# Recurrent mixer: joins and first substitutions over the filled rows only, without clearing the update tiles

## The chip, the cores and the metric

The kernel runs on one core of a Trainium2 chip. The metric is the device time of one execution in microseconds (us). The engines are named as in the profile: PE (TensorE matmuls), PEld (its weight loads), DVE (VectorE), ACT (ScalarE), POOL (GpSimd) and SP (SyncE, whose queue issues the DMAs; SPq in the rows).

## What is computed

The program is a whole two-layer model on 32 samples of 114 positions (1 class token, 36 image patches, 77 text tokens) with 256 channels: a text encoder, a recurrent mixer, routed experts, a state mixer and a factorised MLP. Only the recurrent mixer matters here. Its reference is a scan over the positions:

```python
mixed = silu(causal_conv4(hidden @ W_qkv.T));  z = hidden @ W_z.T
beta = sigmoid(hidden @ W_b.T);  g = -exp(A_log) * softplus(hidden @ W_a.T + dt_bias)
def step(Sst, inp):                     # per sample and head, Sst is 64 x 64
    q_t, k_t, v_t, g_t, b_t = inp
    Sst = Sst * exp(g_t)
    delta = (v_t - Sst.T @ k_t) * b_t
    Sst = Sst + outer(k_t, delta)
    return Sst, Sst.T @ q_t
out = rmsnorm(o * silu(z)) * norm_weight @ W_out.T
```

There are 8 key heads, 16 value heads and 64 channels per head.

## The kernel before, in words

The scan isn't run step by step. For each sample and head the kernel builds a 114x114 triangular matrix `nt` of decayed key products and solves a triangular system for the updates (`upd`, in the code `x`); the outputs are then one product with the decayed query products `qd`.

The system is solved by blocks of 32 rows (the last has 18). The inverses of the four diagonal blocks of all heads and both samples of a pair (128 blocks) are found on DVE at once, one block per partition, in `ue`, by 30 steps of elimination (`eliminate`, L1248 and L1250: a product into `elim_tmp` and a subtraction). Two diagonal blocks are then joined into one inverse of 64 (or 50) rows: `join` (L1665) multiplies the part of `nt` beside the blocks by a turned inverse that lies in `x`; DVE copies the result into `zs` (`join_read`, L1268); `inverse` (L1678) multiplies by the other inverse; ACT copies it into `ut` (`inverse_read`, L1490). Then come the right sides and the substitutions (`solve`): the first halves, rows 0 to 63 (L1700, 64 columns of weights), the carry of their solution into the second halves (L1690), the second substitutions over rows 64 to 113 (L1700, 50 columns), and the outputs (L1707). ACT copies each of them out of PSUM (L1482, L1498).

In `join`, the two joins of a head are issued in turn: one writes PSUM rows 32 to 63 and the other rows 96 to 113 of the same bank. Both, and the first substitution and the carry too, contract over all 114 rows, so what isn't filled in `x` and `zs` has to be zero. For that POOL clears both `x` tiles (`clear_x`, L1196) and DVE clears a gap in them after the join reads (L1272), and SP's loads of the turned inverses into `x` wait for POOL's clearing (`x_clear`). `CHAINS` are the four groups of eight heads (two samples, two groups), each with PSUM banks of its own.

The order of the work is written out by hand: every engine runs `iteration(p)` for each pair of samples `p` (16 pairs, and two more turns of the pipeline), and semaphores alone couple the engines. In one iteration pair `p` forms its matrices, pair `p-1` is eliminated and solved, pair `p-2` is gated, multiplied by `w_out` and stored, and pair `p+1` is projected and convolved.

- DVE: elimination steps with the units of `nt` and `qm` (L1280, L1287) and the gating of `p-2` (L1295, L1300, L1306) between them; turning of the inverse (L1260); gate products (L1311); join reads; the convolutions `conv` 0 to 3 (L1322), with `silu` (L1329) before the last; four products `gated` (L1335).
- ACT: decays (L1414, L1425), reads of the projections, first taps of the convolutions (`first_tap`, L1452: 0 and 1 before the joins, 2 after the reads of the first substitutions, 3 after those of the second), the copies above, `tanh` (L1458).
- PE: projections (L1601), key products (L1576) and decays (L1589), `output_turn` (L1626) and `output_product` (L1634) of `p-2`, gate products (L1617), turning of the values (L1648), then `join`, `inverse`, `solve`.
- POOL: `query_decay` 0 and 1 (L1187), `gate_power` twice (L1200), `clear_x` twice, `query_decay` 2 to 7, and at the end `mask_blocks` on `ue` (L1206, L1210).
- SP: stores the eliminated blocks to DRAM and loads them back in the layouts of `x` (L1133) and `ut` (L1139).

Of the kernel before, what the change touches and what calls it, by code (L numbers as in the profile page):

```python
# [1014 lines left out]
def delta_net(c, hid, xts):  # L1015
# [14 lines left out]
    with ExitStack() as ctx:  # L1030
        def sb(name, shape, dt=F32):
# [23 lines left out]
         o_mm, og_r, osq_r, ms_r, rms_r, on_r, ot_mm, oT_r, wo_mm, h_r, d_dve, pe_gate, pool_gate, sp_gate, x_clear,  # L1055
         uet_r, vd_out, u_in, zz_mm, zs_r, ww_mm, wr_r, x_gap) = (
# [5 lines left out]
                "ms_ready", "rms_ready", "on_ready", "ot_mm", "oT_ready", "wo_mm", "h_ready", "dve", "pe_gate", "pool_gate", "sp_gate", "x_cleared",  # L1062
                "inverse_turned", "turned_out", "turned_in", "join1_mm", "join1_ready", "join2_mm", "join2_ready", "x_gap_cleared"))
# [23 lines left out]
        with nc.Block() as block:  # L1087

            @block.sync
            def _(sp):  # L1090
# [19 lines left out]
                def iteration(p, a=True, proj=True, z=True, d=True):  # L1110
# [10 lines left out]
                    if z:  # L1121
# [7 lines left out]
                        sp.wait_ge(x_clear, r.n * 2 + 2)  # L1129
# [48 lines left out]
            def _(pool):  # L1178
# [34 lines left out]
                def iteration(p, a=True, proj=True, z=True, d=True):  # L1213
                    r = p.shift(-2)
                    for v in range(4):
                        if a:
                            query_decay(p, 2 * v)
                            query_decay(p, 2 * v + 1)
                        if d and v == 0:
                            gate_power(r, 0)  # L1220
                            gate_power(r, 1)
                        if z and v == 0:
                            clear_x(p.shift(-1), 0)
                            clear_x(p.shift(-1), 1)
                    if a:
                        mask_blocks(p)
# [12 lines left out]
            def _(dve):  # L1239
# [23 lines left out]
                def join_read(r):  # L1263
                    for m, (s, g) in enumerate(CHAINS):
                        dve.wait_ge(zz_mm, r.n * 4 + m + 1)
                        need(dve, ww_mm, r.n * 4 - 3 + m)
                        for _, rows, _ in JOINS:
                            last = dve.tensor_copy(zs[s][rows, hs(g), :], ps[rows, XBANK[m], 0:256].rearrange("p (h c) -> p h c", h=8))  # L1268
                        last.then_inc(zs_r, 1)
# [4 lines left out]
                def unit(p, v):  # L1274

                    s, u = divmod(v, 2)
# [5 lines left out]
                    if v == 0:  # L1282
                        need(dve, p_mm, p.n * 4 - 4)
                        need(dve, nd_out, p.n * 128 - 128)
                    for o in range(2):
                        dve.wait_ge(e_r, p.n * 8 + 2 * v + o + 1)
                        dve.tensor_tensor(  # L1287
                            nt[p.par][s][:, hs(u), :].rearrange("p (a o b) t -> p a o b t", o=2, b=2)[:, :, o],
                            e[o][:, :, :].rearrange("p (a b) t -> p a b t", b=2),
                            kq[:, o, :, 1, :].unsqueeze(2).to_broadcast([S, 2, 2, S]), ALU.mult).then_inc(nt_r, 1)  # L1290
# [22 lines left out]
                def conv(r, n):  # L1313

                    dve.wait_ge(tap_r, r.n * 4 + n + 1)
                    for k in range(1, TAPS):
                        for i in range(4):
                            t = 4 * n + i
                            y = yqk[:, t, :, :] if t < 8 else yv[r.par][:, t - 8, :, :]
                            if k > 1:  # L1320
                                dve.wait_ge(conv_r, r.n * 48 + 12 * n + 4 * (k - 2) + i + 1)
                            dve.scalar_tensor_tensor(y, raw[:, t, :, k:k + S], taps[:, t, k:k + 1], y, ALU.mult, ALU.add).then_inc(conv_r, 1)  # L1322
# [14 lines left out]
                def iteration(p, a=True, proj=True, z=True, d=True):  # L1337
# [3 lines left out]
                    if a:  # L1341
                        unit(p, 0)
# [5 lines left out]
                    if a:  # L1348
                        unit(p, 1)
# [9 lines left out]
                    if a:  # L1359
                        unit(p, 2)  # L1360
                    if z:
                        eliminate(r, 20, BW - 1)
# [6 lines left out]
                    if a:  # L1369
                        unit(p, 3)  # L1370
# [3 lines left out]
                    if z:  # L1374
                        join_read(r)
                    if proj:
                        conv(nxt, 0)
                        conv(nxt, 1)
                        conv(nxt, 2)
                        silu(nxt, 0)  # L1380
                        conv(nxt, 3)
# [4 lines left out]
                    if z:  # L1386
                        for m in range(1, 4):
                            gated(r, m)
# [15 lines left out]
            def _(act):  # L1404
# [13 lines left out]
                def decay_terms(p, v):  # L1418

                    s, u = divmod(v, 2)  # L1420
                    for o in range(2):
                        need(act, dec_mm, p.n * 8 + 2 * v + o - 1)
                        for m in range(4):
                            head = 8 * u + 4 * (m // 2) + 2 * o + m % 2
                            last = act.activation(gl[o][:, m, :], c.upto[:, :], ACT.Copy,  # L1425
                                                  scale=gates[:, bass.ds(p.sample(s), 1), head:head + 1].rearrange("p a h -> p (a h)"))
                        last.then_inc(gl_r, 1)
# [46 lines left out]
                def rhs_read(r, q):  # L1474
                    rows = HALVES[q]
                    for m, (s, g) in enumerate(CHAINS):
                        if q == 0:
                            act.wait_ge(vt_mm, r.n * 4 + m + 1)
                            act.wait_ge(zz_mm, r.n * 4 + m + 1)
                        else:  # L1480
                            act.wait_ge(p_mm, r.n * 4 + m + 1)
                        act.copy(x[s][rows, hs(g), :], ps[rows, VBANK[m], :].rearrange("p (h d) -> p h d", h=8)).then_inc(rc_r, 1)  # L1482

                def inverse_read(r):

                    for m, (s, g) in enumerate(CHAINS):
                        act.wait_ge(ww_mm, r.n * 4 + m + 1)
                        need(act, t_mm, r.n * 8 - 3 + m)
                        for rows, cols, _ in JOINS:
                            last = act.copy(ut[s][rows, hs(g), cols],  # L1490
                                            ps[rows, XBANK[m], 256:].rearrange("p (h c) -> p h c", h=8)[:, :, 0:cols.stop - cols.start])
                        last.then_inc(wr_r, 1)

                def x_read(r, q):
                    rows = HALVES[q]
                    for m, (s, g) in enumerate(CHAINS):
                        act.wait_ge(t_mm, r.n * 8 + 4 * q + m + 1)
                        act.copy(x[s][rows, hs(g), :], ps[rows, XBANK[m], :].rearrange("p (h d) -> p h d", h=8)).then_inc(xc_r, 1)  # L1498

                def iteration(p, a=True, proj=True, z=True, d=True):  # L1500
                    r, done, nxt = p.shift(-1), p.shift(-2), p.shift(1)

                    def raws(lo, hi):
                        if proj:
                            for f in range(lo, hi):
                                raw_read(nxt, f)

                    def exps(v):
                        if a:
                            decay_exp(p, 2 * v)  # L1510
                            decay_exp(p, 2 * v + 1)
                            if v < 3:
                                decay_terms(p, v + 1)

# [3 lines left out]
                    exps(0)  # L1518
                    raws(0, 4)
                    exps(1)  # L1520
                    raws(4, 6)
# [3 lines left out]
                    exps(2)  # L1525
                    raws(6, 8)
# [3 lines left out]
                    exps(3)  # L1530
# [3 lines left out]
                    if proj:  # L1534
                        decay_terms(nxt, 0)
                        first_tap(nxt, 0)
                        first_tap(nxt, 1)
                    if z:
                        rhs_read(r, 0)
                        inverse_read(r)  # L1540
                        x_read(r, 0)
# [1474 lines left out]
```

## Time and profile before

| | |
|---|---|
| median of 3 runs | 3087.56 us (3084.33 to 3089.98) |
| profiled execution | 3085.63 us |
| its span in the trace | 3083.9 us |
| PE, DVE, ACT, POOL busy in the span | 79%, 68%, 40%, 26% |
| mean granted PE clock | 0.881 |

The mixer's iterations lie between about 880 and 2160 us of the span. Busy shares are averages over all stages; the profile's clock is a share of the full 2.4 GHz, of which two levels are granted, 1.00 and 0.50 (1.2 GHz). A granted clock between them in a row is a mean over a stretch that had both. In a timeline row the bracket is the idle time of that engine before the row and what ended it. A float32 matmul of the code is two MATMUL records, so the 64 matmuls of the joins are x128. Times in the rows are from the start of the span.

### The profile page before, as it was taken

How to read it: one execution, taken by the hardware profiler on the slowest of the kernel's cores; microseconds unless marked ns; L12 is line 12 of the kernel's file. 1: busy time of each engine (PE TensorE's matmuls, PEld its weight loads, DVE VectorE, ACT ScalarE, POOL GpSimd, SP SyncE). 2: the span in 40 equal slices, each digit the busy share in tenths (PEclk: the TensorE clock that was granted, in tenths of full speed). 3: DMA queues.
4: the chain of work that ended last, by engine and by line, in shares of the span. 5: the costliest groups of instructions: out<-in, count | busy, mean ns of one | idle time of the engine just before them, and what ended most of it. 6: DMA issues, size and time to landing. Idle time of an engine off the chain costs nothing. (4 is left out here: it accounts for less than half of the span.)

```text
span 3083.9 us, 53608 instructions
## 1 busy us (share of the span) xinstructions
PE 2436.0 (79%) x19286; PEld 1864.6 (60%) x19286; DVE 2084.8 (68%) x5004; ACT 1244.2 (40%) x2990; POOL 815.8 (26%) x644
## 2 busy tenths in 40 slices
PE   7888887997458888888888888876452847889698
PEld 5666665886446666666666666655341735566454
DVE  4777774333368888888888888855563336876663
ACT  1334342221256566666666666642000213344132
POOL 2111100001033232232222333221377036450110
PEclk9999998997579999999999999988665877899799
DMA  4210001002201111211122211111211852110000
GB/s 141 72 62 27 12 9 45 21 27 75 100 19 46 49 49 49 50 49 50 49 50 49 50 49 49 46 46 30 88 45 21 263 176 63 45 51 4 18 25 25
DMA packets 274346, 169.01 MB, mean 55 GB/s; under 512 B 182847, under 2 KB 250318, under 8 KB 273728
## 3 DMA queue, kind: packets, MB, share of 16 engines
q1 hardware_dynamic: 247949, 140.28, 15.9%
q0 software_dynamic: 26112, 25.03, 3.1%
q8 instruction: 166, 2.72, 0.4%
q14 instruction: 119, 0.97, 0.1%
HBM read 99.23 MB, written 73.45 MB: 56 GB/s over the span
## 5 line engine op out<-in xcount | busy, mean ns | idle before, releaser
L1187 POOL TENSOR_TENSOR qd<-decay,qm 114x456 f32<-114x456 f32 x128 | 143.4, 1141 | 638.3 <-DVE qm L1280 492.5
L1601 PE MATMUL d_ps<-d_xT,w_qkv 128*128 128x228 f32 x1024 | 236.8, 391 | 44.7 <-DVE qmask L1395 29.2
L1601 PEld LDWEIGHTS d_ps<-d_xT,w_qkv 128*128 128x128 f32 x1024 | 217.2, 213 | 77.1 <-issue 43.2
L2256 POOL DMA_INDIRECT s_eo<-rows_y,slots_all x128 | 152.4, 1191 | 148.3 <-POOLq L87 110.3
L1248 DVE TENSOR_TENSOR elim_tmp<-ue 128x30 f32<-128x30 f32 (+14 forms) x480 | 178.8, 372 | 13.8
L1250 DVE TENSOR_TENSOR ue<-ue,elim_tmp 128x30 f32<-128x30 f32 (+14 forms) x480 | 171.9, 358 | 16.5
L475 PE MATMUL t_ps<-xT,w_qk 128*128 128x154 f32 x1024 | 151.1, 300 | 40.3 <-DVE qk L308 30.9
L1589 PE MATMUL d_ps<-gl,after 114*114 114x456 f32 x256 | 137.2, 654 | 47.2 <-DVE sz L1335 47.2
L1322 DVE SCALAR_TENSOR_TENSOR y_v<-raw,taps,y_v 128x228 f32<-128x228 f32 x384 | 167.1, 508 | 10.6 <-ACT y_v L1452 10.5
L475 PEld LDWEIGHTS t_ps<-xT,w_qk 128*128 128x128 f32 x1024 | 136.7, 189 | 51.8 <-DVE qk L308 38.1
L1206 POOL TENSOR_SCALAR_AFFINE_SELECT ue<-ue 128x1024 f32<-128x1024 f32 x16 | 98.6, 6162 | 238.1 <-DMA ue<-blocks_n 238.1
L1414 ACT ACTIVATE decay<-d_ps,gates 114x114 f32<-114x114 f32 x512 | 133.1, 372 | 64.9 <-PE d_ps L1589 64.5
L1847 POOL DMA_INDIRECT rows_x<-r_xn,slot x128 | 144.3, 1128 | 51.1 <-issue 36.7
L1322 DVE SCALAR_TENSOR_TENSOR y_qk<-raw,taps,y_qk 128x228 f32<-128x228 f32 x384 | 142.2, 450 | 22.0 <-ACT y_qk L1452 21.6
L1425 ACT ACTIVATE gl<-upto,gates 114x114 f32<-114x114 f32 x512 | 151.6, 416 | 0.0
L1634 PE MATMUL d_ps<-w_out,oT 128*114 128x256 f32 x512 | 126.9, 404 | 16.3 <-ACT oT L1471 16.3
L1700 PE MATMUL d_ps<-upd,ut 114*50 114x64 f32 (+1 forms) x2048 | 130.5, 227 | 2.9 <-issue 2.4
L1700 PEld LDWEIGHTS d_ps<-upd,ut 114*50 114x50 f32 (+1 forms) x2048 | 126.5, 138 | 6.2 <-issue 5.7
L1617 PE MATMUL d_ps<-w_z,d_xz 128*114 128x512 f32 x256 | 121.4, 619 | 10.7 <-DVE sz L1311 9.6
L1634 PEld LDWEIGHTS d_ps<-w_out,oT 128*114 128x114 f32 x512 | 95.9, 190 | 46.5 <-ACT oT L1471 20.6
L276 POOL TENSOR_TENSOR rstd<-rstd,minus_half 77x1 f32<-77x1 f32 x32 | 23.4, 732 | 377.2 <-DVE rstd L291 377.2
L415 ACT COPY pT<-t_ps 77x462 f32<-77x462 f32 (+1 forms) x96 | 44.8, 498 | 191.2 <-PE t_ps L525 186.5
(343 smaller groups left out, 5625.0 us busy)
## 6 DMA issues: line engine op xcount, KB each, us to landing
rows_x<-zero_row SPq DMA_DIRECT2D x4, 2048.0 KB, 7.7
ue<-blocks_n SPq DMA_DIRECT2D x16, 512.0 KB, 4.9
blocks_u<-ue SPq DMA_DIRECT2D x16, 512.0 KB, 2.6
blocks_v<-on SPq DMA_DIRECT2D x16, 512.0 KB, 2.7
e_x<-rows_x SPq DMA_DIRECT2D x32, 256.0 KB, 4.3
e_gu<-L_ffn_w_gate_up SPq DMA_DIRECT2D x32, 256.0 KB, 4.3
rows_y<-e_y SPq DMA_DIRECT2D x32, 256.0 KB, 3.4
blocks_n<-nt SPq DMA_DIRECT2D x96, 64.0 KB
```

Source lines behind the costliest of these rows:

```text
L475: last = pe.matmul(ps[:, 6 + f % 3 % 2, (t - lo) * P2:(t - lo + 1) * P2], w_qk[:, k, t * 128:(t + 1) * 128], xT[pair % 3][:, k, :], start= ...
L1187: pool.tensor_tensor(qd[p.par][s][:, hs(u), :].rearrange("p (a o b) t -> p a o b t", o=2, b=2)[:, :, o], e[o][:, :, :].rearrange("p (a b) ...
L1248: ch(dve.tensor_tensor(part, ue[:, j, j + 1:].unsqueeze(1).to_broadcast([128, j, BW - 1 - j]), ue[:, 0:j, j:j + 1].to_broadcast([128, j, B ...
L1250: step = dve.tensor_tensor(ue[:, 0:j, j + 1:], ue[:, 0:j, j + 1:], part, ALU.subtract)
L1322: dve.scalar_tensor_tensor(y, raw[:, t, :, k:k + S], taps[:, t, k:k + 1], y, ALU.mult, ALU.add).then_inc(conv_r, 1)
L1425: last = act.activation(gl[o][:, m, :], c.upto[:, :], ACT.Copy, scale=gates[:, bass.ds(p.sample(s), 1), head:head + 1].rearrange("p a h -> ...
L1589: pe.matmul(ps[0:S, 4 + o, 0:4 * S].rearrange("p (h t) -> p h t", h=4), c.after[:, :], gl[o][:, :, :], start=True, stop=True).then_inc(dec ...
L1601: last = pe.matmul(ps[:, f % 2, (t % 2) * W:(t % 2 + 1) * W], w_qkv[:, k, t * 128:(t + 1) * 128], xT[:, k, :], start=(k == 0), stop=(k == ...
L1634: last = pe.matmul(ps[0:S, 6, 0:D], oT[:, k, :], w_out[:, k, :], start=(k == 0), stop=(k == 7))
L1700: last = pe.matmul(ps[rows, XBANK[m], i * DH:(i + 1) * DH], ut[s][:, 8 * g + i, rows], x[s][:, 8 * g + i, :], start=True, stop=True)
L1847: pool.indirect_dma_start(out=rows_x, out_offset=bass.IndirectOffsetOnAxis(ap=slot[g % 3][:, s, k:k + 1], axis=0), in_=xn[g % 3][:, s, :], ...
L2256: pool.indirect_dma_start(out=eo[n % EO][:, s * TOPK + k, :], out_offset=None, in_=rows_y, in_offset=bass.IndirectOffsetOnAxis(ap=slots_al ...
```

## The change

- `join` becomes `join_part`: each of the two joins of a head contracts only over the 32 rows that are filled (rows 0 to 31, or 64 to 95). The eight matmuls of one join of a group follow each other, and the other join follows later, behind a wait for the first one's end.
- The first substitutions and the carries contract over rows 0 to 63 alone (`known`, `HALVES[0]`). The inverse's second product, the second substitutions and the outputs are as before.
- `clear_x` on POOL and the clearing of the gap on DVE, with their semaphores, are gone. SP's loads into `x` wait for the outputs of the pair before (`o_mm`) instead.
- Everything else in the diff writes loops out by hand in the order that they had.

```diff
 # SP
-                        sp.wait_ge(x_clear, r.n * 2 + 2)
+                        need(sp, o_mm, r.n * 4)
 # POOL
-                def clear_x(r, s):
-                    need(pool, o_mm, r.n * 4 - 2 + 2 * s)
-                    pool.sem_inc(pool_gate, 1)
-                    pool.memset(x[s][:, :, :], 0.0).then_inc(x_clear, 1)
 # DVE, end of join_read
-                    for s in range(2):
-                        rows, _, o = JOINS[1]
-                        dve.memset(x[s][rows, :, o:o + BW], 0.0).then_inc(x_gap, 1)
 # PE
-                        for i in range(8):
-                            for _, rows, o in JOINS:
-                                last = pe.matmul(ps[rows, XBANK[m], i * BW:(i + 1) * BW], nt[r.par][s][:, 8 * g + i, rows],
-                                                 x[s][:, 8 * g + i, o:o + BW], start=True, stop=True)
-                        last.then_inc(zz_mm, 1)
+                def join_part(r, m, n):
+                    s, g = CHAINS[m]
+                    lower, rows, o = JOINS[n]
+                    for i in range(8):
+                        last = pe.matmul(ps[rows, XBANK[m], i * BW:(i + 1) * BW], nt[r.par][s][lower, 8 * g + i, rows],
+                                         x[s][lower, 8 * g + i, o:o + BW], start=True, stop=True)
+                    last.then_inc(zz_mm if n else za_mm, 1)
+                def join_second(r, m):
+                    pe.wait_ge(za_mm, r.n * 4 + m + 1)
+                    pe.sem_inc(pe_gate, 1)
+                    join_part(r, m, 1)
+                # substitute(r, q, m)
+                    known = HALVES[0] if q == 0 else slice(0, S)
+                        last = pe.matmul(ps[rows, XBANK[m], i * DH:(i + 1) * DH], ut[s][known, 8 * g + i, rows],
+                                         x[s][known, 8 * g + i, :], start=True, stop=True)
+                # carry(r, m)
+                        last = pe.matmul(ps[HALVES[1], VBANK[m], i * DH:(i + 1) * DH], nt[r.par][s][HALVES[0], 8 * g + i, HALVES[1]],
+                                         x[s][HALVES[0], 8 * g + i, :], start=False, stop=True, skip_group_check=True)
+                # order on PE
+                        join_first(r, 0, a)
+                        join_first(r, 1, a)
+                        join_second(r, 0)
+                        join_second(r, 1)
+                        join_first(r, 2, a)
+                        join_first(r, 3, a)
+                        join_second(r, 2)
+                        join_second(r, 3)
```

`JOINS` is `[(slice(0, 32), slice(32, 64), 0), (slice(64, 96), slice(96, 114), 32)]`.

## Rows read from the trace of the kernel before

**Rows 1.** Windows, one iteration: busy time and records by engine, granted clock.

```profile
1223.80:1301.90 78.10, 67.08 (x705) 53.04 (x704) 68.25 (x151) 48.35 (x125) 21.59 (x14) 0.94 0.20 49
```

**Rows 2.** Timeline of that iteration, from the elimination's end to the inverse.

```profile
1259.83 0.21 DVE L1250 TENSOR_TENSOR ue<-ue,elim_tmp 128x30 f32<-128x30 f32 x1
...
1264.23 1.91 SPq L1133 DMA_DIRECT2D upd<-blocks_v  x4
...
1269.12 2.18 PE L1665 MATMUL d_ps<-upd,nt 114*32 114x32 f32 x128 [1.01 <-DMA upd<-blocks_v]
1269.92 3.54 DVE L1268 COPY join<-d_ps 32x256 f32<-32x256 f32 x8 [2.52 <-PE d_ps L1665]
...
1273.62 1.03 DVE L1272 MEMSET upd<- 32x512 f32 x2 [0.16 <-issue]
1274.12 3.30 PE L1678 MATMUL d_ps<-ut,join 114*32 114x32 f32 x128 [2.82 <-DMA ut<-blocks_u]
```

**Rows 3.** Timeline, its substitutions and the convolutions beside them.

```profile
1277.35 4.06 PE L1700 MATMUL d_ps<-upd,ut 114*64 114x64 f32 x61
...
1281.40 3.57 PE L1690 MATMUL d_ps<-upd,nt 114*50 114x64 f32 x61
...
1282.11 1.61 ACT L1452 ACTIVATE y_v<-raw,taps 128x228 f32<-128x228 f32 x4
...
1283.75 6.21 DVE L1322 SCALAR_TENSOR_TENSOR y_v<-raw,taps,y_v 128x228 f32<-128x228 f32 x12 [0.19 <-ACT y_v L1452]
...
1284.81 3.74 PE L1700 MATMUL d_ps<-upd,ut 114*50 114x64 f32 x64
...
1291.85 4.47 DVE L1322 SCALAR_TENSOR_TENSOR y_v<-raw,taps,y_v 128x228 f32<-128x228 f32 x12
```

**Rows 4.** Waits between 1000 and 1800 us (ten iterations): total, times, longest.

```profile
DVE y_v L1322 <- ACT y_v L1452: 8.3, 7, 5.0
```

**Rows 5.** Timeline, POOL's clearing and what follows it on POOL, DVE and PE.

```profile
1237.12 1.84 POOL L1196 MEMSET upd<- 114x1024 f32 x2
...
1238.92 2.75 POOL L1187 TENSOR_TENSOR qd<-decay,qm 114x456 f32<-114x456 f32 x2
...
1239.47 1.27 DVE L1248 TENSOR_TENSOR elim_tmp<-ue 128x234 f32<-128x234 f32 x1
...
1240.78 1.16 DVE L1250 TENSOR_TENSOR ue<-ue,elim_tmp 128x234 f32<-128x234 f32 x1
1241.97 0.41 DVE L1248 TENSOR_TENSOR elim_tmp<-ue 128x238 f32<-128x238 f32 x1
...
1241.55 3.71 PE L1634 MATMUL d_ps<-w_out,oT 128*114 128x256 f32 x16 [0.94 <-ACT oT L1471]
...
1245.77 0.41 DVE L1306 TENSOR_TENSOR d_h<-d_h,d_ps 114x256 f32<-114x256 f32 x1
```

**Rows 6.** Timeline, text attention: matmuls with PSUM rows 0 and 64 in turn.

```profile
318.08 1.30 PE L537 MATMUL t_ps<-pT,v 77*64 77x77 f32 x32
```

**Rows 7.** Timeline, last stage: 128 and 16 rows contracted, 456 columns streamed.

```profile
2952.37 1.71 PE L2902 MATMUL f_ps<-f_xT,f_in 128*128 128x456 f32 x4
2955.73 1.79 PE L2910 MATMUL f_ps<-f_aT,f_c 16*128 16x456 f32 x4
...
2931.02 3.40 PE L2910 MATMUL f_ps<-f_aT,f_c 16*128 16x456 f32 x4
```

**Rows 8.** Windows: PE first, granted clock third from the end.

```profile
2930.20:2933.40 3.20, 3.20 (x6) 1.30 (x5) 0.69 (x1) 0.46 (x1) 0.00 (x0) 0.50 0.28 83
...
1274.70:1277.90 3.20, 3.20 (x108) 3.16 (x103) 3.20 (x9) 2.33 (x8) 0.00 (x0) 0.50 0.63 138
...
1039.20:1049.20 10.00, 7.77 (x138) 7.54 (x134) 8.22 (x23) 3.60 (x10) 3.29 (x2) 0.50 0.42 137
```

**Rows 9.** Timeline of the iteration in which the clock stayed low longest.

```profile
1043.91 6.20 PE L1700 MATMUL d_ps<-upd,ut 114*64 114x64 f32 x61
...
1052.45 4.49 DVE L1322 SCALAR_TENSOR_TENSOR y_v<-raw,taps,y_v 128x228 f32<-128x228 f32 x12 [5.03 <-ACT y_v L1452]
```

More of the change, by code:

```diff
@@ L1213, in iteration @@
                 def iteration(p, a=True, proj=True, z=True, d=True):
[L1214 to L1224, printed above, removed]
-                    if a:
+                    r, done, nxt = p.shift(-1), p.shift(-2), p.shift(1)
+                    if a:
+                        query_decay(p, 0)
+                        query_decay(p, 1)
+                    if d:
+                        gate_power(done, 0)
+                        gate_power(done, 1)
+                    if a:
+                        query_decay(p, 2)
+                        query_decay(p, 3)
+                        query_decay(p, 4)
+                        query_decay(p, 5)
+                        query_decay(p, 6)
+                        query_decay(p, 7)
                         mask_blocks(p)
@@ L1386, in iteration @@
                     if z:
-                        for m in range(1, 4):
-                            gated(r, m)
+                        gated(r, 1)
+                        gated(r, 2)
+                        gated(r, 3)
                     ch.end()
@@ L1472, in oT_read @@
                                        ACT.Copy, scale=gain[:, :]).then_inc(oT_r, 1)
[L1474 to L1498, printed above, removed]
+                def rhs_read(r, q, m):
+                    rows, (s, g) = HALVES[q], CHAINS[m]
+                    if q == 0:
+                        act.wait_ge(vt_mm, r.n * 4 + m + 1)
+                        act.wait_ge(zz_mm, r.n * 4 + m + 1)
+                    else:
+                        act.wait_ge(p_mm, r.n * 4 + m + 1)
+                    act.copy(x[s][rows, hs(g), :], ps[rows, VBANK[m], :].rearrange("p (h d) -> p h d", h=8)).then_inc(rc_r, 1)
@@ L1669, in inverse @@
-                def inverse(r):
-                    for m, (s, g) in enumerate(CHAINS):
-                        if m == 0:
-                            pe.wait_ge(ut_in, r.n * 128 + 128)
-                        pe.wait_ge(zs_r, r.n * 4 + m + 1)
-                        pe.sem_inc(pe_gate, 1)
-                        for i in range(8):
-                            for rows, cols, _ in JOINS:
-                                last = pe.matmul(ps[rows, XBANK[m], 256 + i * BW:256 + i * BW + cols.stop - cols.start],
-                                                 zs[s][:, 8 * g + i, :], ut[s][:, 8 * g + i, cols], start=True, stop=True)
-                        last.then_inc(ww_mm, 1)
@@ new lines, in value @@
+                def value(r, m, a):
+                    s, g = CHAINS[m]
+                    if m == 0:
+                        pe.wait_ge(yy_r, r.n * 2 + 2)
+                    if s:
+                        pe.wait_ge(sz_r, r.n * 4 + 3 + g)
+                    elif a:
+                        pe.wait_ge(e_r, r.n * 8 + 15 + g)
+                    else:
+                        need(pe, og_r, r.n * 4 - 3 + g)
+                    for t in range(4):
+                        last = pe.matmul(ps[0:S, VBANK[m], t * 128:(t + 1) * 128], yv[r.par][:, 4 * g + t, s, :], c.ident[:, :],
+                                         start=(t == 0), stop=True, is_transpose=True, skip_group_check=True)
+                    last.then_inc(vt_mm, 1)
@@ new lines, in join_second, with inverse @@
+                def join_second(r, m):
+                    pe.wait_ge(za_mm, r.n * 4 + m + 1)
+                    pe.sem_inc(pe_gate, 1)
+                    join_part(r, m, 1)
+                def inverse(r, m):
+                    s, g = CHAINS[m]
+                    if m == 0:
+                        pe.wait_ge(ut_in, r.n * 128 + 128)
+                    pe.wait_ge(zs_r, r.n * 4 + m + 1)
+                    pe.sem_inc(pe_gate, 1)
+                    for i in range(8):
+                        for rows, cols, _ in JOINS:
+                            last = pe.matmul(ps[rows, XBANK[m], 256 + i * BW:256 + i * BW + cols.stop - cols.start],
+                                             zs[s][:, 8 * g + i, :], ut[s][:, 8 * g + i, cols], start=True, stop=True)
+                    last.then_inc(ww_mm, 1)
@@ new lines, in outputs @@
+                def outputs(r, m):
+                    s, g = CHAINS[m]
+                    if m == 0:
+                        pe.wait_ge(qd_r, r.n * 8 + 8)
+                        pe.sem_inc(pe_gate, 1)
+                    pe.wait_ge(xc_r, r.n * 8 + 4 + m + 1)
+                    for i in range(8):
+                        last = pe.matmul(ps[0:S, VBANK[m], i * DH:(i + 1) * DH], qd[r.par][s][:, 8 * g + i, :],
+                                         x[s][:, 8 * g + i, :], start=True, stop=True)
+                    last.then_inc(o_mm, 1)
```

361 lines of the change are left out of this document (214 added, 147 removed).

## Prediction

> **What bounds the kernel now.** I read the windows of one iteration first, then its timeline, then the waits. In 78.1 us DVE is busy for 68.3 and PE for 67.1 [rows 1], so neither engine is full, and the question is which waits come last in an iteration. The elimination ends on DVE at 1260.04; the blocks go to DRAM and come back, the joins start 9.1 us later (the DMA into `upd` ends PE's wait) and the inverse 14.1 us later (the DMA into `ut` ends a wait of 2.8 us) [rows 2]. After the first substitutions ACT reads, makes the first tap of convolution 2, and DVE starts that convolution 0.03 us behind it, having waited 0.19 [rows 3]. In ten iterations DVE waits there 7 times, 8.3 us in all [rows 4]. So two paths from the elimination's end reach convolution 2 at nearly the same time: DVE's own (join reads, clearing, convolutions 0 and 1) and DMA, inverse, first substitutions, ACT. Saving on one of them alone saves little; lengthening the second is paid in full. From convolution 2 to the next elimination's end it is DVE's own work that counts, with convolution 3 waiting in the same way for the second substitutions: it starts 3.3 us after they end [rows 3], of which reads and tap on ACT take about 2.7.
>
> **The clearing, and SP's wait.** POOL's two clearings end at 1238.96, and the load into `upd` is issued at 1264.23, when the stored blocks have landed [rows 2, 5]: the load waits for something else, and the outputs of the pair before, for which it is to wait now, are older still. No gain, no cost. Two clearings of the gap take DVE 1.03 us, with the gap ahead of them 1.2 [rows 2].
>
> What POOL does 1.84 us sooner is `query_decay` 2 and 3 [rows 5]. Behind them two elimination steps took 1.27 and 1.16 us where the next took 0.41: 1.6 us lost while POOL read SBUF. Earlier by up to 1.8 us, these two overlap units that read PSUM and the scaling of the gated outputs instead. I expect one of the two collisions to remain. But DVE then meets another wait: the residual (L1306) needs `output_product`, which ends at 1245.26, only 0.5 us before the residual starts today, and whose own start (the scaling) doesn't move. So the gain is between 0 and 0.5 us; I take 0.3, over 14 iterations 4 us. The Trainium skill ("SBUF — State Buffer", section "Who interferes with whom") says that a DVE instruction with two SBUF inputs contends with a GpSimd instruction that reads SBUF and not with one that only writes; the trace agrees, with 1.16 to 1.27 us beside `query_decay` against 0.41. By it alone, with no residual to wait for, the term would be 1.6 x 14 = 22 us.
>
> **The joins.** The contraction over fewer rows saves no time by itself: four matmul records of 456 columns take 1.79 us with 16 rows and 1.71 us with 128 [rows 7]. The order costs. Today two places of PSUM rows alternate, and a record takes 2.18/128 = 17 ns, 0.53 ns a column; the attention, with two places in turn, has 1.30/32 = 41 ns for 77 columns, also 0.53 [rows 2, 6]. The carries, all in one place, take 3.57/61 = 59 ns for 64 columns, 0.91 ns [rows 3]. The new joins write one place eight times in a row: 32 x 0.91 = 29 ns a record, 128 of them 3.7 us instead of 2.2. The ends are 2.2 (no loss) and 7.4 (29 ns doubled at the low clock). At 3.7 PE still ends 1.3 us before `ut` arrives. DVE's first read needs 48 records instead of 32 and comes some 0.8 us later, the last ends about 0.95 later; with 1.2 less for the clearing DVE is 0.25 us ahead at convolution 2, where it waits for ACT anyway: 0 now, at most 0.25 x 16 = 4 us if ACT were in time. The wait for the first join's end has eight matmuls of another group before it and costs nothing. Substitutions and carries keep their columns and records: no change at the same clock.
>
> **PE's clock.** This is the term that decides. The inverse's 3.30 us fell in a stretch at 0.50 (1.2 GHz), after PE had mostly waited for `ut` [rows 2, 8]; the clock is low there in about half of the iterations and is back for the substitutions. The inverse contracts over 114 rows. What the clock did when PE was busy with few rows is shown in the last stage: at 2930.2 to 2933.4 PE was busy without a gap, from 2931.0 on with records of 16 rows, and the clock stayed at 0.50, the four records taking 3.40 us instead of 1.79 [rows 7, 8]. I conclude that few rows count for little in what lifts the clock or holds it. After the change PE has, before the inverse, 3.7 us of 32-row joins between two waits, and behind it 7.6 us of 64-row matmuls. So I expect the clock to fall in or before the inverse in every iteration, and, unless the inverse alone lifts it at once, to stay low through substitutions and carries, up to the second substitutions with their 114 rows.
>
> The trace has one iteration to price that by: the clock was at 0.50 from 1039.2 to 1049.2, 61 records of the first substitutions took 6.20 us, 102 ns each, and DVE waited 5.03 us at convolution 2 [rows 8, 9]. In terms of the iteration of rows 2 and 3: the inverse ends at 1277.4 as now; first substitutions 64 x 102 ns = 6.5, to 1283.9 (now 1281.4); convolution 2 at 1286.2 (+2.5). Carries slowed by the same 102/58: 6.5 us, to 1290.4; second substitutions, at the low clock for two thirds of their way, 5.6 us, to 1296.0 (now 1288.5); ACT 2.7 us; convolution 3 at 1298.7 instead of 1291.85. That is +6.8, less a little that DVE saves because POOL's masking no longer falls beside convolution 2: 6.5 us for an iteration in which the clock stays low. Where it comes back with the inverse, the start of the fall within the joins still costs 0 to 1.3 us; I take 0.5. How many are of each kind depends on where the fall starts, which differs from one iteration to the next; since it starts earlier than today, before the inverse rather than over it, I take 10 of the 16 as staying low.
>
> **Sum.** 10 x 6.5 + 6 x 0.5 - 4 = +64 us. The profiled execution took 3085.6 us (1.7 us around its span of 3083.9) and lies 1.9 below the median of the runs, so the median goes from 3087.6 to about 3151. With 4 or with 16 such iterations the sum is +28 or +100, and if each costs 7.5 us, the latter +116: 3115 to 3203.
>
> **Rivals.**
> - *PE kept busy keeps its clock.* If busy time counts, whatever the rows, joins of 3.7 us fill the wait before the inverse and the clock no longer falls there. Then the 8.3 us per ten iterations [rows 4] go, 13 over 16; DVE's 0.25 counts, 4; and the 4 of POOL: -21, 3066. For it: the one traced stretch where few rows kept the clock low is short, and the fall now comes after a real idle time. Against it: that stretch had no gap at all [rows 8]. The Trainium skill ("TensorE: Matmul & The Clock Gate", section "Part 1: The HAM clock gate") says that the hardware sets the clock by how busy PE has been; it does not speak of rows. By it the time would be this rival's; the stretch at 2930.2 does not agree with it.
> - *Nothing but POOL's part moves.* Falls as often and as long as today, joins hidden behind the DMA: -4, 3083. For it: 1.3 us of slack before `ut`. Against it: PE's work around the wait changes in kind.
> - *The inverse mostly restores the clock.* It did so in the iteration of rows 2, where the low stretch ended with it. 4 iterations stay low and 12 cost 0.7: +26 + 8 - 4 = +30, 3118.
> - *Worse than forecast.* The joins run at the low clock from their start (7.4 us): the inverse starts 2.4 us after `ut` arrives and DVE's reads end 3 us later, in most iterations, some 1.5 us an iteration, on top of 12 that stay low: 12 x 6.5 + 16 x 1.5 - 4 = +98, 3185.
>
> **Chances.** Forecast 0.65, the inverse restores 0.12, worse 0.07, POOL alone 0.06, clock kept 0.10. A measurement of this kernel tells about 0.2%, 6 us, from no change. The first three are slower: 0.84. POOL alone is no change but for 0.01: 0.05. Faster: 0.11. The range 3092 to 3195 takes in the forecast with counts from 4 to nearly 16 and most of the worse case, and leaves out the two cases below, 0.16.
>
> **What would show each step.** In the windows of the new kernel, the clock at 0.50 over the first substitutions and carries in most iterations, and a mixer stage with a mean clock below the 0.94 of this iteration. 102 ns or so for a record of the first substitutions. DVE's waits for ACT at convolutions 2 and 3 of several us each in such iterations, against 8.3 in all before. The joins at 3.7 us, or about 7 where the clock is low. One elimination step of about 1.2 us beside `query_decay` instead of two, and no clearing on POOL and DVE. The forecast is wrong if the substitutions keep 58 ns a record: then few rows don't hold the clock down, and the time is near 3066 or 3083. If they are slow and the time is still within 0.5%, something I take for the path isn't.

## The result, and the profile after

| | before | after |
|---|---|---|
| median | 3086.54 us (4 runs, 3084.33 to 3089.98) | 3159.43 us (4 runs, 3143.67 to 3163.63) |
| profiled execution, span | 3085.63, 3083.9 us | 3163.63, 3161.9 us |
| mean granted PE clock | 0.881 | 0.850 |

The new kernel is slower: the ratio is 1.0235, 95% interval 1.021 to 1.0259. The forecast was 3151 us with a range of 3092 to 3195.

Windows of two neighbouring iterations of the kernel after, each from one elimination's end to the next, answer to [rows 1]. Columns: window, its length, busy time and records of PE, PEld, DVE, ACT and POOL, granted clock, DMA share, GB/s.

```profile
1280.70:1358.00 77.30, 70.90 (x706) 56.36 (x706) 66.61 (x147) 48.31 (x125) 20.81 (x12) 0.91 0.20 50
1358.00:1440.70 82.70, 75.73 (x706) 61.88 (x706) 65.07 (x147) 48.79 (x125) 19.94 (x12) 0.86 0.18 45
```

The engines do the same work in both; the second is 5.4 us longer. PE is "busy" for 75.7 us of it instead of 67.1 before, which looks like more work and is the same work at another clock. The timeline shows where that is. These rows answer to [rows 2, 3]:

```profile
1365.97 3.79 PE L1698 MATMUL d_ps<-upd,nt 32*32 32x32 f32 x128
...
1367.64 3.53 DVE L1264 COPY join<-d_ps 32x256 f32<-32x256 f32 x8 [2.31 <-PE d_ps L1698]
...
1369.79 1.94 PE L1729 MATMUL d_ps<-ut,join 114*32 114x32 f32 x65
...
1372.12 1.90 PE L1729 MATMUL d_ps<-ut,join 114*32 114x32 f32 x63 [0.39 <-issue]
...
1373.95 6.77 PE L1742 MATMUL d_ps<-upd,ut 64*64 64x64 f32 x61
1380.77 6.71 PE L1752 MATMUL d_ps<-upd,nt 64*50 64x64 f32 x61
1381.56 1.61 ACT L1470 ACTIVATE y_v<-raw,taps 128x228 f32<-128x228 f32 x4
1383.20 4.49 DVE L1321 SCALAR_TENSOR_TENSOR y_v<-raw,taps,y_v 128x228 f32<-128x228 f32 x12 [3.10 <-ACT y_v L1470]
1387.40 5.02 PE L1742 MATMUL d_ps<-upd,ut 114*50 114x64 f32 x64
...
1394.72 4.49 DVE L1321 SCALAR_TENSOR_TENSOR y_v<-raw,taps,y_v 128x228 f32<-128x228 f32 x12 [2.78 <-ACT y_v L1470]
```

The elimination ended at 1357.95. The joins take 3.79 us instead of 2.18, and the inverse starts right behind them, without the 2.82 us of waiting for `ut` that it had. Then 61 records of the first substitutions take 6.77 us instead of 4.06, and the carries 6.71 instead of 3.57. DVE waits 3.10 us at convolution 2 and 2.78 at convolution 3. The windows over the five stretches (joins, inverse, first substitutions, carries, second substitutions) say why; they answer to [rows 8]:

```profile
1366.00:1369.70 3.70, 3.70 (x129) 3.61 (x128) 1.97 (x5) 3.70 (x12) 0.00 (x0) 0.98 0.78 121
1369.80:1373.90 4.10, 3.71 (x128) 3.62 (x128) 4.01 (x12) 3.73 (x11) 0.00 (x0) 0.50 0.57 111
1374.00:1380.50 6.50, 6.50 (x63) 6.50 (x64) 6.10 (x17) 2.37 (x5) 2.67 (x1) 0.50 0.45 161
1380.70:1387.40 6.70, 6.70 (x68) 6.57 (x64) 4.20 (x12) 3.83 (x8) 1.80 (x2) 0.50 0.00 0
1387.50:1392.20 4.70, 4.70 (x63) 4.70 (x64) 2.25 (x2) 4.05 (x5) 0.00 (x0) 0.73 0.00 0
```

PE has not one idle moment from 1374.0 to 1392.2, and its clock is at 0.50 until the second substitutions, over 114 rows, are under way. In 13 of the 16 iterations the carries ran at 0.50 from end to end; before, in none. From one iteration's joins to the next it is 84.6 us with low carries (mean of 11) and 77.0 for the three others; before it was 78.1 (mean of 14; the last two end with the stage and are left out). What decides between the two kinds isn't shown: from the joins' start to the first substitutions PE had no wait over 0.3 us in the three, and none in three of the thirteen either. The waits in the same stretch as [rows 4] (total, times, longest), first ACT's waits for the substitutions in the kernel before, then ACT's and DVE's in the kernel after:

```profile
ACT upd L1498 <- PE d_ps L1700: 19.4, 36, 1.3
```

```profile
ACT upd L1514 <- PE d_ps L1742: 45.2, 58, 1.3
DVE y_v L1321 <- ACT y_v L1470: 44.5, 15, 4.3
```

DVE's 8.3 us of [rows 4] have become 44.5. Where the clearing was, on POOL and DVE, answering to [rows 5]:

```profile
1335.76 3.09 POOL L1187 TENSOR_TENSOR qd<-decay,qm 114x456 f32<-114x456 f32 x2 [0.25 <-DVE qm L1273]
...
1337.84 1.27 DVE L1244 TENSOR_TENSOR elim_tmp<-ue 128x234 f32<-128x234 f32 x1
1339.14 0.40 DVE L1246 TENSOR_TENSOR ue<-ue,elim_tmp 128x234 f32<-128x234 f32 x1
...
1343.69 0.42 DVE L1305 TENSOR_TENSOR d_h<-d_h,d_ps 114x256 f32<-114x256 f32 x1 [0.23 <-PE d_ps L1674]
```

One slow elimination step is left of two, and the residual now waits for `output_product`.

### The profile page after: what moved, and what is told of

It is laid out like the page before. It is cut to its first block and busy times, and to the rows that moved or that the text cites. A ratio compares the mean times of both kernels' runs of the same rounds, so it can differ in the third digit from the quotient of the medians.

```text
span 3161.9 us, 53594 instructions
## 1 busy us (share of the span) xinstructions
PE 2561.9 (81%) x19286; PEld 1999.8 (63%) x19286; DVE 2045.4 (65%) x4972; ACT 1250.2 (40%) x2990; POOL 757.8 (24%) x612
## 5 line engine op out<-in xcount | busy, mean ns | idle before, releaser
L1641 PE MATMUL d_ps<-d_xT,w_qkv 128*128 128x228 f32 x1024 | 229.1, 382 | 54.3 <-DVE qmask L1413 29.7
L1641 PEld LDWEIGHTS d_ps<-d_xT,w_qkv 128*128 128x128 f32 x1024 | 210.5, 207 | 84.0 <-issue 42.7
L1321 DVE SCALAR_TENSOR_TENSOR y_v<-raw,taps,y_v 128x228 f32<-128x228 f32 x384 | 150.6, 468 | 78.9 <-ACT y_v L1470 78.9
L1742 PE MATMUL d_ps<-upd,ut 114*50 114x64 f32 (+1 forms) x2048 | 191.6, 281 | 0.1
L1742 PEld LDWEIGHTS d_ps<-upd,ut 114*50 114x50 f32 (+1 forms) x2048 | 186.3, 187 | 2.9 <-issue 0.2
L475 PE MATMUL t_ps<-xT,w_qk 128*128 128x154 f32 x1024 | 151.1, 300 | 40.2 <-DVE qk L308 30.9
L1246 DVE TENSOR_TENSOR ue<-ue,elim_tmp 128x30 f32<-128x30 f32 (+14 forms) x480 | 161.5, 336 | 16.5
L1200 POOL TENSOR_SCALAR_AFFINE_SELECT ue<-ue 128x1024 f32<-128x1024 f32 x16 | 65.8, 4110 | 231.9 <-DMA ue<-blocks_n 231.9
L510 PE MATMUL t_ps<-w_v,xT 128*77 128x512 f32 x256 | 118.3, 606 | 0.0
```

The source lines that it names most:

```text
L475: last = pe.matmul(ps[:, 6 + f % 3 % 2, (t - lo) * P2:(t - lo + 1) * P2], w_qk[:, k, t * 128:(t + 1) * 128], xT[pair % 3][:, k, :], start= ...
L1246: step = dve.tensor_tensor(ue[:, 0:j, j + 1:], ue[:, 0:j, j + 1:], part, ALU.subtract)
L1641: last = pe.matmul(ps[:, f % 2, (t % 2) * W:(t % 2 + 1) * W], w_qkv[:, k, t * 128:(t + 1) * 128], xT[:, k, :], start=(k == 0), stop=(k == ...
L1742: last = pe.matmul(ps[rows, XBANK[m], i * DH:(i + 1) * DH], ut[s][known, 8 * g + i, rows], x[s][known, 8 * g + i, :], start=True, stop=True)
```

## The experiments

The theory: how many rows a matmul contracts over counts in PE's clock, so joins over 32 rows let it fall before the inverse, and substitutions and carries over 64 keep it low. The rivals: the new matmuls or their new order are slow in themselves; busy time alone sets the clock; leaving the clearing out costs. The table has all kernels. "Inverse low" is the share of the inverse's time at 0.50, the mean of 16 iterations of the profiled execution; "carries low" counts the iterations with the carries at 0.50. Ratios are to the kernel before, run on the same chip in the same series.

| kernel | rows of joins / first substitutions and carries | clearing | inverse low | carries low | median, us | ratio, 95% interval |
|---|---|---|---|---|---|---|
| before | 114 / 114 | yes | 0.37 | 0 | 3085 to 3087 | 1 |
| after | 32 / 64 | no | 0.96 | 13 | 3159.4 | 1.0235 (1.021, 1.0259) |
| order_only | 114 / 114 | yes | 0.04 | 0 | 3099.7 | 1.0048 (1.003, 1.0066) |
| joins_few | 32 / 114 | yes | 0.96 | 0 | 3098.4 | 1.0056 (1.0031, 1.0081) |
| subs_few | 114 / 64 | yes | 0.06 | 10 | 3151.6 | 1.0229 (1.0172, 1.0286) |
| after_clears | 32 / 64 | yes | 0.95 | 12 | 3173.7 | 1.0297 (1.0249, 1.0345) |
| after_filled | 32 / 64, four matmuls of 128 rows added | no | 0.28 | 2 | 3118.0 | 1.0116 (1.0065, 1.0167) |
| few_filled | 32 / 64, four matmuls of 32 rows added | no | 1.00 | 8 | 3167.7 | 1.0292 (1.0237, 1.0346) |
| gap_pool | as before | gap on POOL | 0.41 | 0 | 3070.3 | 0.9955 (0.9939, 0.9971) |
| gap_pool_filled | as before, four of 128 added | gap on POOL | 0.01 | 0 | 3065.4 | 0.9934 (0.9909, 0.9959) |
| qd_early | as before | later | 0.45 | 0 | 3082.6 | 0.9989 (0.9975, 1.0004) |
| best | as gap_pool_filled | later, gap on POOL | 0.00 | 0 | 3056.6 | 0.9909 (0.989, 0.9928) |

**order_only.** The new kernel with these edits, and the clearing put back:

```diff
-    last = pe.matmul(ps[rows, XBANK[m], i * BW:(i + 1) * BW], nt[r.par][s][lower, 8 * g + i, rows],
-                     x[s][lower, 8 * g + i, o:o + BW], start=True, stop=True)
+    last = pe.matmul(ps[rows, XBANK[m], i * BW:(i + 1) * BW], nt[r.par][s][:, 8 * g + i, rows],
+                     x[s][:, 8 * g + i, o:o + BW], start=True, stop=True)
-    known = HALVES[0] if q == 0 else slice(0, S)
+    known = slice(0, S)
```

(and `:` for `HALVES[0]` in the contraction of `carry`.)

> The new kernel with the contraction over all rows everywhere and with the clearing of the update tiles on GpSimd and VectorE put back: of the change only the new order of the joins (eight matmuls of one place of PSUM rows in a row) and its waits are left. Theory (few-row matmuls don't hold or lift TensorE's clock): within 6 us of the kernel before, 3080 to 3093, the joins 3.7 us instead of 2.2, the granted clock low in no more iterations than before (mean about 0.88). Rival 1 (the new order, with its later join reads, is what costs): near 3150. Rival 2 (leaving the clearing out costs, by moving GpSimd's query_decay under other work): as the theory, since the clearing is there.

The clock did as expected, but the time is 15 us up, not within 6. The rows of one quiet iteration, whose elimination ended at 1338.2 here and also in the kernel before, show what my expectation had left out: VectorE's own path. Before:

```profile
1347.01 3.54 DVE L1268 COPY join<-d_ps 32x256 f32<-32x256 f32 x8 [1.47 <-PE d_ps L1665]
1350.70 1.03 DVE L1272 MEMSET upd<- 32x512 f32 x2 [0.16 <-issue]
...
1366.93 6.48 DVE L1322 SCALAR_TENSOR_TENSOR y_v<-raw,taps,y_v 128x228 f32<-128x228 f32 x12
```

order_only:

```profile
1346.23 3.77 PE L1710 MATMUL d_ps<-upd,nt 114*32 114x32 f32 x128
1347.91 3.54 DVE L1273 COPY join<-d_ps 32x256 f32<-32x256 f32 x8 [2.31 <-PE d_ps L1710]
1351.61 1.02 DVE L1396 MEMSET upd<- 32x512 f32 x2 [0.16 <-issue]
...
1367.85 6.48 DVE L1330 SCALAR_TENSOR_TENSOR y_v<-raw,taps,y_v 128x228 f32<-128x228 f32 x12
```

The reads start 0.90 us later and convolution 3 by 0.92. That is one quiet iteration. Over 14 iterations of the profiled executions the last instruction of convolution 3 starts 36.35 us after the elimination's end instead of 35.72, 0.63 later, and from there to the next elimination's end it is 42.92 us instead of 42.48, with 44.4 to 45.2 in four iterations (at most 44.2 before). So some 16 x 0.63 = 10 us lie where the later reads are; the cause of the rest stays open. The joins last 3.77 us over 114 rows and 3.79 over 32, so rows don't change a matmul's time; the order does.

**joins_few.** As order_only, with `lower` kept in the joins.

> As order_only, with the joins over their 32 filled rows and everything else over all rows, clearing kept. Theory: the clock falls before or at the inverse in nearly every iteration, but the first substitutions over all 128 rows lift it within a few us; 0.5 to 2 us an iteration, 3095 to 3120, mean clock between 0.86 and 0.88. Rival 1 (few rows are slow in the substitutions alone, whatever the clock): as order_only, within 6 us of before. Rival 2 (busy time counts, rows don't): joins keep PE as busy as in order_only, so the same time as order_only.

Windows over the joins and over the inverse, first of order_only, then of joins_few:

```profile
1346.20:1349.90 3.70, 3.70 (x129) 3.65 (x128) 1.90 (x5) 3.70 (x12) 0.00 (x0) 1.00 0.77 121
1350.00:1353.00 3.00, 2.47 (x129) 2.35 (x130) 2.69 (x7) 2.95 (x9) 0.00 (x0) 1.00 0.40 54
```

```profile
1349.60:1353.30 3.70, 3.70 (x130) 3.58 (x128) 2.19 (x6) 3.70 (x12) 0.00 (x0) 0.94 0.77 119
1353.50:1356.80 3.30, 3.30 (x127) 3.21 (x123) 3.01 (x8) 3.21 (x10) 0.00 (x0) 0.59 0.33 42
```

PE is busy for the whole 3.70 us of the joins in both. With 114 rows the inverse behind them runs at 1.00, with 32 rows mostly at 0.50, and so in all iterations (0.04 against 0.96). That rules busy time out. No cost of it by itself is shown, 3098 against 3100: behind the substitutions over 114 rows the clock is back for the carries in all 16 iterations.

**subs_few.** As order_only, with the first substitutions and the carries over rows 0 to 63.

> As order_only, with the first substitutions and the carries over rows 0 to 63 and the joins over all rows, clearing kept. Theory: the clock falls no more often than before (about half of the iterations, over the inverse), but where it has fallen it now stays low to the second substitutions: 8 iterations x about 5 us, 3110 to 3140, first substitutions 102 ns a record in these and 58 in the others. Rival 1 (64-row matmuls slow in themselves): 102 ns a record in every iteration, near 3160. Rival 2 (busy time counts): as order_only.

52 us above order_only, more than expected. In both traces PE had stood idle inside the inverse just before (first order_only, then subs_few):

```profile
1433.13 0.87 PE L1741 MATMUL d_ps<-ut,join 114*32 114x32 f32 x43 [2.62 <-issue]
```

```profile
1292.91 0.87 PE L1741 MATMUL d_ps<-ut,join 114*32 114x32 f32 x43 [2.35 <-issue]
```

Windows over the first substitutions and the carries, of order_only and then of subs_few:

```profile
1433.90:1438.90 5.00, 5.00 (x64) 4.97 (x59) 5.00 (x15) 2.44 (x6) 1.10 (x1) 0.66 0.58 196
1439.00:1442.50 3.50, 3.50 (x70) 3.50 (x68) 2.43 (x7) 3.12 (x8) 3.27 (x2) 1.00 0.03 7
```

```profile
1293.70:1299.00 5.30, 5.30 (x64) 5.29 (x60) 5.30 (x15) 2.63 (x6) 1.53 (x1) 0.62 0.53 180
1299.30:1306.00 6.70, 6.70 (x69) 6.66 (x66) 5.45 (x13) 3.83 (x8) 3.96 (x2) 0.50 0.01 4
```

In both the clock falls within the first substitutions. Over 114 rows it is back for the carries, over 64 it isn't. In the six other iterations the carries over 64 rows took 3.8 to 4.1 us from the first record's start to the last one's end, against 7.06 in the ten; over 114 rows (order_only) it is 3.8, once 4.7: they aren't slow in themselves. This edit holds nearly all of the loss; with the narrow joins added to it (after_clears) the median is 22 us higher, which lies within the two intervals. It was larger than I expected because only three of the ten low stretches began in the inverse and seven within the substitutions, behind an inverse that had run at 1.00. The narrow substitutions aren't shown to start them: in order_only such a stretch also began in the inverse or the first substitutions, in 7 of 16 iterations, and in both kernels in or behind a wait of PE there (1.6 to 3.3 us in order_only, 1.4 to 3.6 in subs_few). What differs is the end: over 114 rows the clock was back for the carries in all seven, over 64 rows in none of the ten.

**after_filled and few_filled.** The new kernel with matmuls of 128 rows, or of 32, between the last join and the inverse:

```diff
+    def filler(n):
+        for i in range(n):
+            pe.matmul(ps[0:32, 3, 256:512], c.ident[:, 0:32], w_qkv[:, 0, 0:256], start=True, stop=True)
...
      join_second(r, 3)
+    filler(4)
```

few_filled has `c.ident[0:32, 0:32]` and `w_qkv[0:32, 0, 0:256]` in it.

> The new kernel with four more matmuls, 128 rows by 256 columns into PSUM places that nobody reads, between the last join and the inverse, where TensorE waits for the DMA into ut. Nothing else is changed. Theory: with all rows in use just ahead of the inverse the clock is at 2.4 GHz at the inverse and over the substitutions in most iterations: 3070 to 3110, mean clock 0.87 or more, substitutions 58 ns a record. Rival 1 (few-row matmuls or the new order are slow in themselves): the added matmuls help nothing, 3155 to 3165 or more. Rival 2 (leaving the clearing out costs): 3155 to 3165.

> As after_filled, but the four added matmuls contract over rows 0 to 31 instead of all 128: the same places, the same 256 columns, the same count, so TensorE is as long busy with them. Theory (rows in use count): they neither hold nor lift the clock; low over first substitutions and carries in about 13 of 16 iterations as in the new kernel, and the inverse a little later: 3155 to 3180, mean clock 0.85. Rival (busy time counts, whatever the rows): as after_filled, 3100 to 3125, mean clock about 0.876, the substitutions at 58 ns a record in nearly all iterations.

Windows over the added matmuls and the inverse, of after_filled and then of few_filled:

```profile
1358.80:1361.40 2.60, 2.60 (x10) 1.08 (x9) 2.51 (x8) 1.96 (x5) 0.00 (x0) 0.50 0.36 52
1361.50:1364.20 2.70, 2.70 (x132) 2.31 (x130) 2.70 (x8) 1.28 (x5) 0.00 (x0) 0.94 0.68 160
```

```profile
1378.50:1381.60 3.10, 3.10 (x10) 1.00 (x6) 3.01 (x9) 2.08 (x5) 0.00 (x0) 0.50 0.52 76
1381.70:1385.10 3.40, 3.40 (x128) 3.38 (x128) 3.40 (x10) 1.75 (x6) 0.00 (x0) 0.50 0.86 261
```

More work made the kernel 41 us faster by the medians (by the two ratios 37 with an uncertainty of 17), and the same work over a quarter of the rows didn't. after_filled is above my range of 3070 to 3110, since here the inverse hardly waits for `ut` any more, and with the added matmuls it starts later, 14.5 us after the elimination's end instead of 12.8 (means of 16). (Its profiled execution, 3097.8 us, is the fastest of its runs, so its clock columns flatter it.) For few_filled the time came as expected and the count didn't: 8 iterations with low carries, not 13. The inverse ran there without a gap for 3.6 us at 0.50, and the clock was back behind its 114 rows in the other 8 (why in these isn't shown); but a low iteration took 88 us instead of 84.6.

**after_clears.** The new kernel with only the clearing and its waits put back.

> The new kernel with only the clearing put back (GpSimd's two clearings of the update tiles, VectorE's two of the gap, and the waits on them); few rows and the new order of the joins stay. Theory: where the clock stays low VectorE waits for ScalarE at convolution 2 anyway and the clearing is hidden; in the two or three other iterations it costs 1.2 us each, and GpSimd's query_decay comes later again, 4 us: 3159 to 3170, that is 0 to 10 above the new kernel. Rival (leaving the clearing out is itself what slows the new kernel): clearly below the new kernel, 3110 or less.

14 us above the new kernel and just above the expected range, by the two ratios 19 with an uncertainty of 17: the rival is out, and leaving the clearing out helped, if barely beyond the noise. In the low iterations the last instruction of convolution 3 starts 42.4 us after the elimination's end with the clearing and 42.5 without (means over 10 and 11): hidden. Of the others, the quietest has 35.64 and 34.46: 1.2 us.

**gap_pool, gap_pool_filled.** Since DVE's 1.2 us count wherever the clock doesn't rule, and POOL has been idle since `query_decay` 7 at that time, the gap is cleared on POOL (for each `s`, ahead of `mask_blocks`, each instruction behind the end of the one before), in the kernel before:

```diff
-    dve.memset(x[s][rows, :, o:o + BW], 0.0).then_inc(x_gap, 1)
+    pool.wait_ge(zz_mm, r.n * 4 + 2 * s + 2)
...
+    pool.memset(x[s][rows, :, o:o + BW], 0.0).then_inc(x_gap, 1)
```

> The kernel before with one edit: the clearing of the gap (two memsets of 32 rows) is made by GpSimd, between its last query_decay and its masking, instead of by VectorE between the join reads and convolution 0. Joins, substitutions and carries over all rows, old order. Theory: 1.19 us leave VectorE's path in each iteration; in those where ScalarE's tap for convolution 2 is in time (about half) convolution 3 ends about 1.1 us earlier, in the others nothing: 3072 to 3082, and the clock as before, 0.88. Rival (VectorE isn't on the path, the time between elimination and convolution 2 is set by the DMAs and TensorE alone): within 3 us of before.

> As gap_pool, with the four full-row matmuls of after_filled between the joins and the inverse, while TensorE waits for the DMA into ut. Theory: the clock is at 2.4 GHz at the inverse and over the first substitutions in nearly all iterations, so that VectorE's 1.19 us count in nearly all of them: 3062 to 3074, mean clock 0.89 or more. Rival (the added matmuls end after ut has landed and delay the inverse, as in after_filled where it started at 14.4 us behind the elimination's end instead of 12): 3080 to 3095, VectorE waiting for ScalarE at convolution 2 in most iterations.

gap_pool is 0.45% faster than before, just below its range; the last instruction of convolution 3 starts 34.7 us after the elimination's end instead of 35.7 (means of 14). The added matmuls bring the inverse to 2.4 GHz in all but one iteration; that they gain something on top (3065.4 against 3070.3) is within the two intervals, so not shown by these two alone. The mean clock was 0.885, not the 0.89 expected.

**qd_early, best.** `query_decay` 2 and 3 ahead of `clear_x` (`if z and v == 1` for `v == 0` in POOL's loop), alone and on top of gap_pool_filled.

> The kernel before with one edit: GpSimd's two clearings of the update tiles come behind query_decay 2 and 3 instead of ahead of them, so these run 1.84 us earlier, as they do in the new kernel. Theory (the prediction's term): one of the two elimination steps beside query_decay falls from 1.16 us to about 0.4, but the residual then waits for output_product, so that 0 to 0.5 us an iteration are gained: 3079 to 3086, 0 to 8 below before. Rival (VectorE's gain of 0.8 us a step reaches the end): 13 us below before, about 3073.

> gap_pool_filled (the old joins over all rows, the gap cleared on GpSimd, four full-row matmuls while TensorE waits for ut) with the edit of qd_early as well. Theory: 3059 to 3068, 0 to 6 below gap_pool_filled and about 0.7% below the kernel before; the clock at 2.4 GHz over the inverse in 14 or more of 16 iterations. Rival (the next limit, convolution 2's wait for ScalarE, takes both gains): no better than gap_pool, 3070.

qd_early: 2.1 us below before, by the ratio 3.4 with an uncertainty of 4.5: small as forecast; the rival's 13 us are out, no gain at all isn't. best is 0.9% faster than the kernel before and 3.3% faster than the new one, just below its expected range; against gap_pool_filled alone the intervals overlap. Its timeline (joins, gap, added matmuls, inverse, convolution 2):

```profile
1338.36 2.13 PE L1680 MATMUL d_ps<-upd,nt 114*32 114x32 f32 x124
...
1339.73 0.52 POOL L1209 MEMSET upd<- 32x512 f32 x1 [3.96 <-PE d_ps L1680]
...
1340.53 1.67 PE L1687 MATMUL d_ps<-w_qkv,ident 128*32 128x256 f32 x7
...
1342.71 2.21 PE L1698 MATMUL d_ps<-ut,join 114*32 114x32 f32 x128 [0.50 <-DMA ut<-blocks_u]
...
1351.57 6.47 DVE L1337 SCALAR_TENSOR_TENSOR y_v<-raw,taps,y_v 128x228 f32<-128x228 f32 x12
```

The old joins are done 2.1 us after they start, the added matmuls use the wait for `ut` and are over 0.5 us before it lands, and convolution 2 waits for nobody.

## Why the prediction was right, by its own steps

- **PE's clock.** The mechanism held: few rows neither hold nor lift it (order_only against joins_few, order_only against subs_few, after_filled against few_filled). The price was right too: low iterations took 84.6 us against 78.1 before, 6.5 each; convolution 2 started 26.1 us after the elimination's end in them and convolution 3 38.5 (means over 11; the forecast's times are 26.2 and 38.7). Part of that is luck, for errors cancelled: the inverse started at 12.7 us and not 14.1, but took 4.3 us and not 3.3, and the first substitutions 7.0 and not 6.5. And the +6.8 was taken from an iteration with a late convolution 3 (31.8 us; mean before 30.9), so that its real delay was 7.6 us, of which DVE got 0.8 back within convolution 3, not 0.3, and 0.3 behind it (the term of `query_decay`, counted apart). The count was mis-sized: 13 and not 10. And "where it comes back with the inverse, +0.5" had the wrong sign: the three others took 77.0 us, 1.1 less than before. 13 x 6.5 - 3 x 1.1 = +81 for the forecast's 10 x 6.5 + 6 x 0.5 - 4 = +64; the profiled executions differ by 78, the medians by 73. Some of the +64 was luck: too few iterations, but no gain counted in the high ones.
- **What I missed in the clock:** that a low stretch needs no narrow joins. subs_few has full-row joins and still 10 iterations with low carries, and order_only has 7 in which the clock fell in the inverse or the first substitutions. I had put the blame for the start on the joins, and 64 rows in the substitutions are enough to make such a stretch long.
- **The joins.** 3.79 us as forecast (3.7), reads 0.9 later (0.8). But PE was to end 1.3 us before `ut` arrives, and in the new kernel `ut` had arrived: by the records of its landings, its last packet came 11.5 to 12.3 us behind the elimination's end in 14 of 16 iterations, and at 12.6 or later in 15 of 16 before. In the rows of one iteration SP issued its eight loads within 3.79 us instead of 4.89. Why the slower joins let the load through sooner was not tried and stays open. In low iterations it counted: in nine of the eleven convolution 2 started 9.25 us behind the first record of the first substitutions, so there an earlier inverse can pass on to convolution 2.
- **The clearing.** Nothing on POOL and for SP, as forecast. DVE's 1.2 us are hidden in low iterations, and against the later reads they leave 0.36 us in a high one (34.46 for convolution 3's last instruction against 34.82 in a quiet iteration before; forecast 0.25). Taken alone, without the new order, they were worth 0.45% (gap_pool).
- **query_decay.** One slow step of 1.27 us left, the next at 0.40 instead of 1.16, and a wait of 0.23 at the residual. The stretch from convolution 3 to the elimination's end was shorter by 0 to 0.4 us, as the 0.3 said. The Trainium skill ("SBUF — State Buffer", "Who interferes with whom") has the collision right: 1.27 us beside `query_decay`, 0.40 without. The 22 us took both slow steps as gone and nothing else as waiting; one stayed, and qd_early gained 2 to 3 us.
- **The rivals.** "PE kept busy keeps its clock": in joins_few PE was busy throughout the joins shown, and the clock was at 0.50 for part or all of the inverse in all 16 iterations. The Trainium skill's sentence that the hardware goes by how busy PE has been ("TensorE: Matmul & The Clock Gate", "Part 1: The HAM clock gate") doesn't tell these runs apart; rows in use do. "The inverse restores it": so in 3 of 16, and in 8 of 16 of few_filled. "Worse": the joins at 0.50 from their start occurred in none; at most 54% of their time ran so.

## What to carry to other kernels

Cutting the contraction rows of a float32 matmul saved no time here (3.77 us at 114 rows, 3.79 at 32) and took PE's clock: before narrowing matmuls that stand next to a wait, look at the granted clock around them, and keep the rows full, with zeros if need be, unless the zeros cost more on the path than the clock. The clearing that such zeros need belongs on an idle engine. And where PE must wait at a place from which the path runs on, full-row matmuls that nobody reads can be worth their time: in the new kernel they were, although they delayed the inverse; in the old one, where they end before the wait does, their gain stayed within the noise.

## What was unexpected of the hardware

- Four added matmuls of 128 rows made the new kernel 41 us faster; the same four over 32 rows made it no faster (8 us slower by the medians, within the noise).
- A record that stays in one place of PSUM rows took 29 ns and one that alternates between two places 17 ns, at 1.00 and with 114 rows in both (order_only's joins, 3.77/128, against [rows 2]).
- The clock stayed at 0.50 for over 17 us, from 1369.8 to beyond 1387.4, over inverse, substitutions and carries, in which PE was idle for 0.4 us. In another iteration (elimination's end at 1518.58) it was 23.9 us, without one wait of PE over 0.3 us.
